# One attention stream of 256 units, all feed-forward tiles last, and the first layer norm made early by ScalarE and kept turned in DRAM

## The reference

```
x = x + attention(layernorm(x), ctx, ctx, mask, wq, wk, wv, wo)
x = x + ffn(layernorm(x), qweight, lut4, bias)

attention: q = rope(x @ wq), k = rope(ctx @ wk), v = ctx @ wv
           32 query heads, 8 key heads (4 query heads share one), 128 wide
           softmax(q k^T / sqrt(128) + mask) v, then @ wo
ffn:       w[o, i] = lut4[o, code of (o, i)], codes of 4 bit planes
           y = x @ w^T + bias
```

## Time and profile before

| | us |
|---|---|
| median of 3 runs | 2559.84 (2558.57 to 2560.38) |
| the profiled execution, its own time | 2562.46 |
| its span in the profile | 2560.6 |
| TensorE busy | 2486.9 (97%) |
| VectorE busy | 1541.1 (60%) |
| ScalarE busy | 1073.4 (42%) |
| GpSimd busy | 446.4 (17%) |

### The profile page before, as it was taken

One profiled execution on the slowest core, in us unless ns is written; L12 is line 12 of the kernel. 1 busy time (PEld: TensorE's weight loads), 2 busy tenths in 40 slices (PEclk: granted clock), 3 DMA queues, 4 the chain that ended last, 5 costly groups with the idle time before them and its releaser, 6 DMA issues.

```text
span 2560.6 us, 36203 instructions
## 1 busy us (share of the span) xinstructions
PE 2486.9 (97%) x13248; PEld 2128.0 (83%) x13248; DVE 1541.1 (60%) x3664; ACT 1073.4 (42%) x2380; POOL 446.4 (17%) x678
## 2 busy tenths in 40 slices
PE   7999997999999999999999989999999999999999
PEld 6888986888888888888887878888888888888877
DVE  7777777655555555555555755555555555555554
ACT  5333334544444444444443144444444444444420
POOL 0000000122222222222222111222222222222221
PEclk9999998999999999999999989999999999999999
DMA  7343444122122122121215231122122121221141
GB/s 228 130 141 130 146 137 152 42 67 67 58 66 67 57 71 58 58 75 58 62 51 185 83 103 34 58 74 67 55 66 58 63 70 58 62 67 58 50 161 50
DMA packets 198639, 213.96 MB, mean 84 GB/s; under 512 B 13632, under 2 KB 153152, under 8 KB 198464
## 3 DMA queue, kind: packets, MB, share of 16 engines
q1 hardware_dynamic: 198464, 211.65, 25.8%
HBM read 161.28 MB, written 50.33 MB: 83 GB/s over the span
## 4 chain that ended last, share of the span: by engine, by line
PE 87%; DVE 5%; ACT 3%; issue 2%; DMA 2%; SPq 1%; POOL 1%; ACTq 0%; DVEq 0%; POOLq 0%
PE bank L621 27%; PE bank L695 26%; PE bank L733 7%; PE bank L646 7%; PE bank L678 6%; PE bank L575 6%; PE bank L666 4%; PE bank L558 4%; DMA w_scratch<-small_split 1%; PE bank L534 1%; DVE residual L1188 1%; DVE row_numbers L1076 1%; ACT probs L943 0%; SPq L355 0%; DVE residual L1384 0%
## 5 line engine op out<-in xcount | busy, mean ns | idle before, releaser
L695 PE MATMUL bank<-weights_split,small_split 128*128 128x512 f32 x3072 | 775.6, 402 | 13.6 <-DVE small_split L1376 13.6
L621 PE MATMUL bank<-acts_split,weights_split 128*128 128x512 f32 (+1 forms) x3456 | 755.3, 370 | 18.5 <-DVE weights_split L1127 11.0
L621 PEld LDWEIGHTS bank<-acts_split,weights_split 128*128 128x128 f32 x3456 | 590.7, 191 | 112.9 <-DVE weights_split L1127 11.4
L695 PEld LDWEIGHTS bank<-weights_split,small_split 128*128 128x128 f32 x3072 | 562.5, 190 | 128.6 <-DVE small_split L1376 10.6
L1507 POOL TENSOR_SCALAR probs<-probs,row_numbers 128x256 f32<-128x256 f32 x512 | 238.6, 479 | 1418.8 <-DVE row_numbers L1366 1418.8
L943 ACT ACTIVATE probs<-probs,row_numbers 128x256 f32<-128x256 f32 x512 | 256.2, 501 | 492.8 <-DVE row_numbers L1361 492.1
L1355 DVE CUSTOM_DVE_ANT_0 probs<-bank,mask_tile 128x256 f32<-128x256 f32 x512 | 196.4, 421 | 210.7 <-PE bank L646 208.8
L1500 POOL TENSOR_TENSOR rope_x<-rope_x,sin_t 128x512 f32<-128x512 f32 (+1 forms) x144 | 169.3, 1176 | 531.3 <-ACT rope_x L905 531.0
L646 PEld LDWEIGHTS bank<-small_split 128*128 128x128 f32 x1536 | 218.5, 191 | 21.5 <-issue 1.7
L1318 DVE SCALAR_TENSOR_TENSOR rope_a<-bank,cos_t 128x512 f32<-128x512 f32 (+1 forms) x144 | 90.9, 631 | 227.8 <-ACT rope_x L905 227.7
L646 PE MATMUL bank<-small_split 128*128 128x256 f32 x1536 | 225.3, 283 | 1.6 <-DVE small_split L1329 1.6
(11 more groups left out here) (81 smaller groups left out, 2334.6 us busy)
## 6 DMA issues: line engine op xcount, KB each, us to landing
raw<-in_L_xattn_wq SPq DMA_DIRECT2D x64, 512.0 KB, 4.4
raw<-in_L_xattn_wo SPq DMA_DIRECT2D x64, 512.0 KB, 3.5
k_scratch<-small_split SPq DMA_DIRECT2D x64, 256.0 KB, 2.1
v_scratch<-small_split SPq DMA_DIRECT2D x32, 512.0 KB, 2.8
small_split<-k_scratch SPq DMA_DIRECT2D x64, 256.0 KB, 2.7
mask_tile<-in_mask_BxSxS_ff SPq DMA_DIRECT2D x64, 256.0 KB, 3.6
small_split<-v_scratch SPq DMA_DIRECT2D x64, 256.0 KB, 2.9
weights_split<-w_scratch SPq DMA_DIRECT2D x16, 1024.0 KB, 7.4
```

Source lines behind the costliest of these rows:

```text
L621: last = pe.matmul(q_ps[:, 0:wide], wq_s[:, h, c, a, :], xT[:, c, m, b * S:b * S + wide], start=c == 0 and i == 0, stop=c == C - 1 and i == 2)
L695: last = pe.matmul(out_ps[part][:, :], o_s[:, a, u % 2 * S + t * P:u % 2 * S + (t + 1) * P], wo_s[:, h, m, n * BANK:(n + 1) * BANK], start ...
```

## The change

Five things, done together:

- **One stream.** The units of both halves follow each other, 256 in 16 rounds; only the very first round has single query jobs. The low parts of half 1's X are not made in place but loaded (below) at units 114 to 129, while the last jobs of round 7 and first of round 8 run; the residual of half 0 is stored to DRAM (`residual_scratch`) at units 120 to 132 and half 1's x rows are loaded in its place.
- **Feed-forward last.** All 16 tiles stand behind the units, those of half 1 first, then those of half 0, whose residual comes back from DRAM one tile at a time after an output is stored. The feed-forward's weights are loaded once.
- **First layer norm on ScalarE.** `load_row` brings 128 rows of x to `ln_row`; ScalarE makes mean, centred rows, the sum of squares (its pass writes `raw` as a by-product), the root, and the scaled rows; VectorE keeps one small sum and four small steps (`row_var`, `row_scale`). TensorE turns them, ScalarE and VectorE split them into `raw` (`x_high`, `x_low`), and `store_row` puts each half row into `x_scratch` by two DMAs of 256 KB. Before `x_high` or `row_square` writes `raw` again, those stores must have landed.
- **Nine of the 16 tiles in stage A**: `K_ROW` gives tiles made in the key phases of batches 1 to 6 (mean at key g=1, centre 2, square 3, root 5, norm 6, turned behind the last key), `V_ROW` tiles made in the value phases of batches 1 to 3 (turned between the third and fourth value product). The other seven are made one a round in rounds 1 to 7: mean, centre and square at the last three units of the round before, root, scale and norm at its first three, and turned in halves at its units 5 and 6 (`SIDE`).
- **X and first query weights in the last batch.** The turned parts are loaded into `acts_split` by DMAs of 512 KB, half of them in the last value phase, half at units 0 to 3. The four first pieces of query weights use four buffers (`raw`, `ln_row` and two of `acc`); the one in `raw` is issued after the last key store and all row stores.

The core of the diff:

```diff
+    K_ROW = {1: 0, 2: 2, 3: 4, 4: 6, 5: 7, 6: 8}
+    V_ROW = {1: 1, 2: 3, 3: 5}
+    A_ROWS = len(K_ROW) + len(V_ROW)
+    NT = NB * TS
+    ROW_ROUND = {e: e - A_ROWS + 1 for e in range(A_ROWS, NT)}
+    SIDE = {UNITS * g + 5 + j: (e, j) for e, g in ROW_ROUND.items() for j in range(2)}
+    ROW_AT = {UNITS * g: e for e, g in ROW_ROUND.items()}
+    FFN_TILES = list(range(HT, NT)) + list(range(HT))
...
+            def load_row(e):
+                sp.wait_ge(x_tr, 2 * e)
+                sp.dma_start(ln_row[:, :], x_tiles[e]).then_inc(row_in, 16)
+            def store_row(e, j):
+                sp.wait_ge(x_lo, 2 * e + j + 1)
+                dst = x_scr[e // HT, e // REP % 2, 4 * j:4 * j + 4].rearrange("c p l (t n) -> t l p c n", n=P)
+                for l in range(2):
+                    done = sp.dma_start(dst[e % REP, l], raw_t[:, l * BANK:(l + 1) * BANK]
+                                        .rearrange("p (c n) -> p c n", n=P))
+                    done.then_inc(x_stored, 16)
+            def load_turned(hf, j, c):
+                sp.dma_start(xT[:, c, :, j * BANK:(j + 1) * BANK].bitcast(F32),
+                             x_scr[hf, j, c]).then_inc(xT_in[j][c // 2], 16)
...
                     if last:
-                        load_rows(0, 1)
-                        load_raw(0, wq_v[0])
+                        for h in range(2):
+                            load_piece(wq_v[2 + h], acc[:, h, :], wq_in[h])
...
+                    if g == 0 and b == 1:
+                        load_row(K_ROW[b])
...
+                if b in K_ROW:
+                    if b in V_ROW:
+                        load_row(V_ROW[b])
+                    elif b + 1 in K_ROW:
+                        load_row(K_ROW[b + 1])
+                    store_row(K_ROW[b], 0)
+                if last:
+                    sp.wait_ge(x_stored, 4 * 16 * A_ROWS)
+                    load_raw(0, wq_v[0])
                 store_values(V0, 0, 0)
                 if not last:
                     sp.wait_ge(dq_step, b * DQ_STEPS + 1)
                     load_planes(b + 1)
+                if b in K_ROW:
+                    store_row(K_ROW[b], 1)
+                if last:
+                    sp.wait_ge(wide_mm, 1 + b * TS * NN + 2)
+                    for c in range(C // 2):
+                        load_turned(0, 0, c)
                 store_values(V1, 1, 0)
...
+                    load_keys(0)
+                if b in V_ROW:
+                    if b + 1 in K_ROW:
+                        load_row(K_ROW[b + 1])
+                    store_row(V_ROW[b], 0)
                 store_values(V3, 1, 1)
...
+            for u in range(NU):
...
+                if u + 5 in ROW_AT:
+                    if u + 5 == UNITS:
+                        sp.wait_ge(w_lo, A_PIECES + 2)
+                    load_row(ROW_AT[u + 5])
+                if u in SIDE:
+                    store_row(*SIDE[u])
...
+                for j in range(2):
+                    c = u - (HALF_UNITS - 14 + 8 * j)
+                    if 0 <= c < C:
+                        if c == 0:
+                            job = JOB_OF[HALF_UNITS - UNITS + 2 * REP * j + REP - 1]
+                            sp.wait_ge(rope_mm, A_ROPES + job + 1)
+                        load_turned(1, j, c)
...
+            for f in range(NT):
+                sp.wait_ge(out_ready, f + 1)
+                sp.dma_start(out_tiles[FFN_TILES[f]], acc[:, f % HT, :]).then_inc(out_stored, 16)
+                if f < HT:
+                    sp.wait_ge(out_stored, 16 * (f + 1))
+                    sp.dma_start(acc[:, f, :], res_scr[f]).then_inc(x_in[f], 16)
+            sp.wait_ge(out_stored, 16 * NT)
...
+                if b in K_ROW:
+                    turn_row(K_ROW[b])
...
-                if last:
-                    turn_rows((0, 1, 0))
                 values(2)
-                if last:
-                    pe.wait_ge(rope_cosd, 2 + A_ROPES)
-                    turn_rows((0, 1, 1))
+                if b in V_ROW:
+                    turn_row(V_ROW[b])
...
+            def row_mean(e):
+                act.wait_ge(row_in, 16 * (e + 1))
+                act.activation(ln_row[:, :], ln_row[:, :], ACT.Copy, scale=-1.0 / D,
+                               accum_out=x_mean).then_inc(row_step, 1)
+            def row_center(e):
+                act.wait_ge(row_step, 3 * e + 1)
+                act.activation(ln_row[:, :], ln_row[:, :], ACT.Identity, scale=-float(D),
+                               bias=x_mean).then_inc(row_step, 1)
+            def row_square(e):
+                act.wait_ge(row_step, 3 * e + 2)
+                act.wait_ge(x_stored, 4 * 16 * e)
+                act.activation(raw, ln_row[:, :], ACT.Square, scale=float(D) ** -0.5,
+                               accum_out=x_var).then_inc(row_step, 1)
+            def row_root(e):
+                act.wait_ge(row_ve, e + 1)
+                act.activation(x_sd, x_ve, ACT.Sqrt).then_inc(row_sd, 1)
+            def row_norm(e):
+                act.wait_ge(row_r, e + 1)
+                act.activation(ln_row[:, :], ln_row[:, :], ACT.Identity, scale=x_r).then_inc(row_ok, 1)
+            def x_high(e, j, src):
+                act.wait_ge(x_tr, 2 * e + j + 1)
+                act.wait_ge(x_stored, 2 * 16 * (2 * e + j))
+                act.activation(x_split[:, HI, :], src[:, :], ACT.Copy).then_inc(x_hi, 1)
...
+                    if b in K_ROW:
+                        if g == 1:
+                            row_mean(K_ROW[b])
+                        if g == 2:
+                            row_center(K_ROW[b])
+                        if g == 3:
+                            row_square(K_ROW[b])
+                        if g == 5:
+                            row_root(K_ROW[b])
+                        if g == 6:
+                            row_norm(K_ROW[b])
                     if g == 1:
...
+                if b in K_ROW:
+                    x_high(K_ROW[b], 0, x_ps[0])
                 if last:
                     split_hi(raw, raw_in, A_TURNS + 1, wq_s[:, 0, :, HI, :])
+                values_high(V0)
+                if b in K_ROW:
+                    x_high(K_ROW[b], 1, x_ps[1])
+                if b in V_ROW:
+                    row_mean(V_ROW[b])
+                    row_center(V_ROW[b])
+                if last:
+                    split_hi(ln_row[:, :], a_raw_in[1], A_TURNS + 1, wq_s[:, 1, :, HI, :])
                 values_high(V1)
+                if b in V_ROW:
...
                 if last:
-                    row_high((0, 1, 0))
+                    for h in range(2):
+                        split_hi(acc[:, h, :], wq_in[h], 1, wq_s[:, 2 + h, :, HI, :])
                 values_high(V2)
...
+            def row_scale(e):
+                dve.wait_ge(row_sd, e + 1)
+                row_scale_steps(x_sd, x_ve, x_y, x_e, x_f, x_r).then_inc(row_r, 1)
+            def x_low(e, j, src):
+                dve.wait_ge(x_hi, 2 * e + j + 1)
+                dve.tensor_tensor(x_split[:, LO, :], src[:, :], x_split[:, HI, :].bitcast(F32),
+                                  ALU.subtract).then_inc(x_lo, 1)
...
+                if b in K_ROW:
+                    x_low(K_ROW[b], 0, x_ps[0])
...
                 leaf(4, B)
+                if last:
+                    query_lo(0)
...
+                if b in K_ROW:
+                    x_low(K_ROW[b], 1, x_ps[1])
...
+                if b in V_ROW:
+                    row_var(V_ROW[b])
+                pick(2, B, C_)
+                if b in V_ROW:
+                    row_scale(V_ROW[b])
+                pick(3, A, B, last=True)
...
+                    x_low(V_ROW[b], 0, x_ps[0])
+                if not last:
```

1102 lines of the change are left out of this document (492 added, 610 removed).

## The result

The changed kernel takes 2537.03 us in the median (2535.62 to 2539.65, 4 runs) against 2559.92 for the kernel before beside it: ratio .9913, 95% interval .9895 to .993, so 22.9 us faster. Forecast were 2529 and 30 us, in a range of 2511 to 2547. The span of the profiled execution fell from 2560.6 to 2534.7, by 25.9.

The account below looks back on a forecast made before the run. TensorE, busy 97% of the span, was taken as the bound. Span 2560.6 - 40.9 - 22.8 + 12.6 + 14.1 + 4.6 + 2.0 = 2530.2; + 1.9 - 2.6 gives 2529 us, range 2511 to 2547.

Parts of the forecast that it names:

- The seam: Unit 120 of half 0 to unit 24 of half 1: 370.3 us becomes 235.0 for units plus 94.4 for tiles, -40.9.
- The start: Last value phase to unit 10: 133.9 us becomes 111.1, -22.8, including a 4.2 wait for the late first query weight.
- Sixteen turned tiles: Transposes of 16 tiles moved into batches 1 to 6 and rounds 1 to 7, .79 us each, +12.6.
- Value-phase rows: Value phases of batches 1 to 3: TensorE waits about 3.0 us for the row, plus 1.7 for clock, three times, +14.1.
- Batch 1: Key phase of batch 1: the row lands late, key products wait 2.9 us plus 1.7 for clock, +4.6.
- the key-phase lag: Batches 2 to 6: ScalarE's mean pass delays the swap in the key phase, .3 to .4 us a batch, +2.0.
- Table loads and sides at nothing: Rounds 1 to 7: ScalarE's 14 function-table loads and the splits of turned tiles cost TensorE nothing.
- the rival that took such a price: Rounds 1 to 7: each table swap costs TensorE 1.4 us, 14 x 1.4 = 20, giving 2549 us; chance .03.
- From span to median: Last step: 1.9 us added to the span for execution time, 2.6 taken off to reach the median.
- hid its rows: Rival in stage A: waits in value phases and batch 1 fall under 1.5 us; 2511, or 2505 with last batch's; chance .14.
- stalled twice as much: Rival in stage A: six key-phase rows each make a second wait of some 3 us, 18 in all, 2547; chance .10.
- the sides: Rival: rows beside units 5 and 6 of rounds 1 to 7 stall TensorE; 27 us (2556), chance .04, or 53 (2583), .06.

Follow-up runs that it names:

- e6_seam: Changed kernel with the loads of half 1's turned rows and residual issued only behind a key load, never just ahead of one: span 2531.8 us against 2534.7.
- e8_bare_rows: Changed kernel with the seven tiles of rounds 1 to 7 made without their layer norm (output differs): span 2534.8 us against 2534.7.
- e1_spare_dump: Changed kernel with the by-product of the squares written to the unused mask tile instead of `raw`: span 2529.6 us against 2534.7.
- e4_wq_early: Changed kernel with the last batch's first piece of query weights loaded ahead of the key phase instead of behind it: span 2529.4 us against 2534.7.
- e3_row1_early: Changed kernel with batch 1's first row of x loaded before the batch's first key store instead of behind it: span 2533.0 us against 2534.7.

## Why the prediction was right, point by point

- **The seam, -40.9:** right; 370.3 became 236.6 + 94.4, -39.3. What was missed are 1.6 us in it at units 131 and 132, and 1.8 outside it at units 115 and 116: the keys land late behind loads of which the prediction said "I cost them at nothing". The condition that it gave was another: that waits in SyncE's queue hold up a key load. Here the keys were issued nearly in time and took 5.5 and 5.7 us to land, against a median of 2.7; e6_seam shows the cause.
- **The start, -22.8:** -21.5. The working holds link by link: the weight's high part started 10.3 us into the phase (forecast 10.1), V0's low part ended at 15.3 (15.2), and the wait was 4.31 (4.2). Its clock was charged 1.7 and cost 3.4, since the half clock lasted 6.8 us (.91 over the 38.6 us of that window). The first query then also waited 1.0 for X, which the sum did not have. Units 0 to 10 took 73.8 against 75.0.
- **Sixteen turned tiles, +12.6:** .8 each in stage A, .90 each in the rounds, 13.5. The side groups of four transposes cost .46 and not .40.
- **Value-phase rows, +14.1:** 5.0, 5.5 and 5.3 over a phase of 21.8 with its transposes, 15.8. Place, engine and size are right, and the 1.7 for the clock was what it cost in each of the three (5.0 against 3.2 + 1.7). The working wasn't all of it: the stores of the first half row hold `x_high` for 4.3 us, and once the stores are out of the chain the last link is VectorE's order; taking out the store wait that was named won 1 to 1.7 each.
- **Batch 1, +4.6, and the key-phase lag, +2.0:** 34.2 - 29.5 - .8 = 3.9, where the wait was the 2.9 of the forecast; and .5 in batch 2, nothing in 3 to 6, .5 in the last: 1.0. The first batch was 1.5 shorter, within what it varies.
- **Table loads and sides at nothing:** right, to a tenth of a microsecond (e8_bare_rows). The Trainium skill (ScalarE: Activation LUTs, What ACT_TABLE_LOAD costs) counts a drain of some 1380 ns beside each load. The trace does not agree: the rows at 576.38 have .01 us ahead of the load and .02 behind it. The 20 us of the rival that took such a price did not come.
- **From span to median:** a step that was wrong. The prediction took off 2.6 us because the profiled execution before was that much above its median. The changed kernel's own was .5 below (2536.52 and 2537.03). Sum and span: -30.4 forecast, -25.9 measured; medians: -30.4 and -22.9. Of the difference of 7.5, 3.0 is this step and 4.5 are the places above.
- **What cancelled:** terms that were too favourable make 7.3 (the loads beside the units 3.4, the start 1.3, tiles .9, value phases 1.7), the key phases were 1.7 too dear, and the first batch was 1.5 shorter, which is luck. The rest, .4, has no place here beyond .1 in each value phase of batches 4 to 6.

The rivals: stage A neither hid its rows nor stalled twice as much; the sides and the table loads did nothing.

## What to carry to other kernels

Work that is moved into a serial chain over several engines and a DMA costs by how late the chain ends for the engine that waits for it, and not by its busy time: the seven layer norms beside the units cost TensorE nothing but their transposes, and three chains that ended 3 to 4 us late cost 16. When one link is taken out, read again which link is next before the gain is booked; here it was a sum of .14 us behind 4 us of work that was less urgent. Issue a load that is needed at once ahead of bulk loads: behind one of 512 KB the keys landed 5.5 us after their issue and without it 3.8, while the DMA engines were only .37 busy over the seam (units 120 to 152).

## What was not expected of the hardware

- Half clock (1.2 of 2.4 GHz) behind a stall does not follow from the stall's length alone. In e1_spare_dump stalls of 2.38 and 1.97 left the granted clock at 1.00 and one of 2.23 brought it to .83 over 10 us. In the changed kernel the stalls of 3.2 to 3.7 were all followed by 3.4 us of half clock, and so was one of 1.83 at the weights' transposes of batch 1 (.83 over 68 to 78). In e4_wq_early one of 3.26 was not; the row, and the stretch around it as a window:

```profile
116.80 1.09 PE L573 MATMUL bank<-ident,ln_row 128*128 128x128 f32 x8 [3.26 <-ACT ln_row L822]
```

```profile
113.00:123.00 10.00, 6.74 (x35) 5.39 (x34) 6.25 (x12) 4.77 (x9) 0.00 (x0) 1.00 0.49 154
```

Behind the stalls of 4.25 and 3.44 in e3_row1_early it lasted 6.8 us. So the prediction's rule, 1.7 for every wait of 2 us and more and nothing below, fitted the three value phases and is no rule of these runs; what decides stays open.
- The eight loads of X in the last value phase, issued in two groups of four and .6 to 1.3 us apart in each, landed 1.3 to 2.7 us apart, 4.8 to 9.3 us after their issue, where a load of 512 KB has a median of 4.4 in the earlier trace rows. The last landed at 434.70, and the query's last six matmuls start at 434.74: that sets how early the first query can run.
